# A decoder layer on one core: the second expert's loads moved behind the attention, and the first batch's gate projection moved behind softplus

## The reference

```
xc, res = split(x @ W_in.T + b_in)                  # 512 channels each
u   = silu(conv3(xc) + conv_b)                      # depthwise, causal, 3 taps
dlt, Bm, Cm = split(u @ W_x.T, [64, 80])            # rank 64, 16 states
delta = softplus(dlt @ W_dt.T + b_dt)
h_t = exp(delta * A) * h_(t-1) + delta * u * Bm     # restarts every 64 tokens
x = layernorm(x + ((h . Cm) * silu(res)) @ W_out.T + b_out)
x = layernorm(x + attention(x, ctx, 16 heads of 16))
x = layernorm(x + experts(x))                       # 8 experts: token t of all
                                                    # sequences goes to expert t // 32
experts: (silu(x @ w1) * (x @ w3)) @ w2             # 704 hidden channels
```

## Time and profile before

| | |
|---|---|
| three runs | 2793.26, 2795.64 (median), 2803.66 us |
| profiled execution | 2792.28 us, its span 2790.5 us |
| busy | PE 2424.6, DVE 2140.0, POOL 2074.5, ACT 1802.9 us |
| mean granted TensorE clock | 0.955 |

### The profile page before, as it was taken

The page is one execution under the profiler, slowest core; times in us unless marked ns, Lnnn a source line. Parts: engine busy times, 40 slices in busy tenths (PEclk is TensorE's granted clock), DMA queues, the critical chain, the costliest instruction groups (busy, mean ns, idle before and its releaser), DMA issues. The chain is left out here.

```text
span 2790.5 us, 49779 instructions
## 1 busy us (share of the span) xinstructions
PE 2424.6 (87%) x14816; PEld 1660.6 (60%) x14816; DVE 2140.0 (77%) x3586; ACT 1802.9 (65%) x3972; POOL 2074.5 (74%) x968
## 2 busy tenths in 40 slices
PE   3578888888889898889889888898888879999998
PEld 2345666666666666666666666666665545555554
DVE  1778999999999999999999999999999832322332
ACT  1666777877888888777877787878777541211111
POOL 2999999999999999999999999999999500000000
PEclk8788999999999999999999999999998879999999
DMA  3456566666666666666666666666666360343221
GB/s 118 128 133 149 150 165 168 165 158 157 157 169 166 160 158 165 165 162 168 166 169 164 162 164 166 165 173 163 166 172 158 86 180 12 91 126 96 78 79 31
DMA packets 319323, 399.65 MB, mean 143 GB/s; under 512 B 115697, under 2 KB 256241, under 8 KB 314962
## 3 DMA queue, kind: packets, MB, share of 16 engines
q1 hardware_dynamic: 303698, 384.91, 53.5%
q10 hardware_dynamic: 15360, 11.55, 1.5%
HBM read 300.86 MB, written 94.37 MB: 142 GB/s over the span
## 5 line engine op out<-in xcount | busy, mean ns | idle before, releaser
L506 POOL TENSOR_TENSOR arena<-arena 128x1024 f32<-128x1024 f32 x512 | 1208.2, 2363 | 66.6 <-DMA arena<-w_dram 42.3
L582 ACT ACTIVATE dA_ps<-arena,a_neg 128x252 f32<-128x252 f32 x2048 | 868.7, 461 | 330.4 <-DVE dA_ps L787 172.0
L764 DVE TENSOR_TENSOR_SCAN arena<-dA_ps,arena 128x512 f32<-128x512 f32 x672 | 803.6, 1208 | 112.5 <-ACT dA_ps L582 88.0
L516 POOL TENSOR_TENSOR arena<-arena 128x1024 f32<-128x1024 f32 (+1 forms) x416 | 808.1, 1943 | 17.8 <-DVE arena L764 17.2
L764 DVE TENSOR_TENSOR_SCAN dA_ps<-dA_ps,arena 128x512 f32<-128x512 f32 x352 | 416.2, 1205 | 3.9 <-POOL arena L506 3.7
L887 PE MATMUL a_ps<-xT,w_conv 128*128 128x256 f32 x1536 | 369.8, 391 | 0.0
L829 DVE TENSOR_REDUCE mx<-s_ps 128x2 f32<-128x512 f32 x497 | 334.0, 672 | 23.2 <-PE s_ps L887 23.2
L887 PEld LDWEIGHTS a_ps<-xT,w_conv 128*128 128x128 f32 x1536 | 288.4, 194 | 54.1 <-issue 16.5
L887 PE MATMUL y_ps<-arena,sel 128*32 128x256 f32 x4096 | 257.5, 393 | 55.5 <-DVE m_rows L835 27.8
L640 ACT ACTIVATE probs<-st_ps 128x512 f32<-128x512 f32 x493 | 285.3, 579 | 29.7 <-PE st_ps L887 25.5
L887 PE MATMUL s_ps<-k_st,q_st 96*128 96x256 f32 x994 | 260.6, 344 | 43.7 <-DVE mx L829 28.0
(11 more groups left out here) (111 smaller groups left out, 3272.9 us busy)
## 6 DMA issues: line engine op xcount, KB each, us to landing
arena<-delta_dram SPq DMA_DIRECT2D x512, 128.0 KB, 2.8
arena<-w_dram SPq DMA_DIRECT2D x512, 128.0 KB, 3.2
arena<-bc_dram SPq DMA_DIRECT2D x128, 256.0 KB, 4.5
q_st<-q_parts_dram SPq DMA_DIRECT2D x512, 64.0 KB
k_st<-k_parts_dram SPq DMA_DIRECT2D x512, 64.0 KB
w_dram<-u SPq DMA_DIRECT2D x32, 512.0 KB, 2.8
delta_dram<-delta SPq DMA_DIRECT2D x32, 512.0 KB, 3.8
k_parts_dram<-parts SPq DMA_DIRECT2D x32, 512.0 KB, 4.0
```

What stands on the lines that cost most here:

```text
L506: pool.tensor_tensor(dBu[:, n % NB], w_r[:, n // RP % 2, t % RP].unsqueeze(1).to_broadcast([P, QS, L]), bc_r[:, b.par, 0], ALU.mult).then_ ...
L516: pool.tensor_tensor(h[:, n % NH, states], h[:, n % NH, states], bc_r[:, b.par, 1, states], ALU.mult).then_inc(s_hC, 1)
L582: last = nc.scalar.activation(dA[n % NDA][:, q, :, 1:], delta_r[:, n // (2 * RP) % 2, t % RP].rearrange("p (c t) -> p c t", t=CH)[:, :, 1: ...
L764: nc.vector.tensor_tensor_scan(dst, decays, dBu[:, n % NB, 2 * half:2 * half + 2].rearrange("p q t -> p (q t)"), 0.0, ALU.mult, ALU.add).t ...
```

## The change

Four edits.

1. Start: SP issues the four bias parts ahead of `w_xc` and `conv_rows`. DVE makes `rows * row_scales` first, and the float32r copy is made by ScalarE.
2. Start: `w_x`, `w_dt` and `w_gate` get a semaphore of their own, `s_front`, and are issued ahead of SP's wait. The first `x_proj` waits for them. The wait for the other seven stands ahead of the first `state_sum`.
3. The first batch's `gate_proj` is issued behind its `dt_proj` on TensorE, and its `gate_evac` and Silu behind its `softplus` on ScalarE, with a load of the Exp and Ln table behind it. The other batches are as before.
4. The mixers load expert 0 alone. Expert 1's `w13`, columns, `w2` and rows are issued at the start of the `experts` block, when all stores have landed; its last columns come from DRAM too, and ScalarE copies them for expert 0 only.

```diff
@@ weights and set-up counts
+        front_weights = [(w_x[:], "w_x"), (w_dt[:], "w_dt"), (w_gate[:], "w_gate")]
         weights = [
-            (w_gate[:], "w_gate"), (w_x[:], "w_x"), (w_dt[:], "w_dt"), (sel[:], "sel"), (w_out[:], "w_out"),
+            (sel[:], "sel"), (w_out[:], "w_out"),
...
-        N_CONV = 6 + NDA + TAPS * KD
+        N_ROWS = 3 + NDA
+        N_CONV = 5 + NDA + TAPS * KD
@@ SP
+            for tile, name in bias_parts:
+                sp.dma_start(tile, io[name]).then_inc(s_bias_ld, 16)
             sp.dma_start(w_xc.rearrange("p q t -> p (q t)"), io["w_xc"]).then_inc(s_conv_ld, 16)
             sp.dma_start(conv_rows, io["conv_rows"].partition_broadcast(P)).then_inc(s_conv_ld, 16)
-            for tile, name in bias_parts:
-                sp.dma_start(tile, io[name]).then_inc(s_bias_ld, 16)
 
             def load_weights():
+                for tile, name in front_weights:
+                    sp.dma_start(tile, io[name]).then_inc(s_front, 16)
+                sp.wait_ge(s_const_v, N_SET)
                 for tile, name in weights:
                     sp.dma_start(tile, io[name]).then_inc(s_const, 16)
-                    sp.wait_ge(s_const_v, N_SET)
                 sp.wait_ge(s_const_p, 4)
...
-                    for e in range(2):
-                        shared.load_columns(sp, e, 0, ET - P)
-                        shared.load_rows(sp, e, 0, EJ - 1)
+                    shared.load_columns(sp, 0, 0, ET - P)
+                    shared.load_rows(sp, 0, 0, EJ - 1)
...
-                *[(O_LD + 11 + 6 * e, load_expert(e, shared.load_w13)) for e in range(2)],
-                *[(O_LD + 14 + 6 * e, load_expert(e, shared.load_w2)) for e in range(2)],
+                (O_LD + 11, load_expert(shared.load_w13)),
+                (O_LD + 14, load_expert(shared.load_w2)),
                 (O_LD + 23, load_tokens),
@@ ScalarE
+            act.wait_ge(s_const_v, N_ROWS)
+            nc.scalar.activation(bias[:], rows, ACT.Copy).then_inc(s_const_a, 1)
             nc.scalar.activation(a_neg[:], a_neg[:], ACT.Exp).then_inc(s_const_a, 1)
...
             def silu(b):
                 act.wait_ge(s_conv, b.value(2, 2))
                 nc.scalar.activation(u[:], u[:], ACT.Silu).then_inc(s_u, 1)
-                act.wait_ge(s_gate, b.value(2, 2))
-                nc.scalar.activation(gate[:, b.par], gate[:, b.par], ACT.Silu).then_inc(s_gsilu, 1)
+                if b.back(1):
+                    silu_gate(b)
                 nc.scalar.preload_act_table_set(EXP_LN)
+
+            def first_gate(b):
+                if not b.back(1):
+                    for half in range(2):
+                        gate_evac(half)(b)
+                    silu_gate(b)
+                    nc.scalar.preload_act_table_set(EXP_LN)
...
-                *[(O_GATE + 4 * half + 2, gate_evac(half)) for half in range(2)],
+                *[(O_GATE + 4 * half + 2, later_gate_evac(half)) for half in range(2)],
+                (O_SP + 2, first_gate),
@@ DVE
+            dve.wait_ge(s_bias_ld, 16 * len(bias_parts))
+            nc.vector.tensor_tensor(rows, rows, row_scales, ALU.mult).then_inc(s_const_v, 1)
             dve.wait_ge(s_conv_ld, 32)
...
-            dve.wait_ge(s_const_v, N_CONV - 3)
-            nc.vector.tensor_copy(bias[:], rows).then_inc(s_const_v, 1)
-            dve.wait_ge(s_const_v, N_CONV - 2)
+            dve.wait_ge(s_const_a, 1)
@@ TensorE
-                    if m == 0 and not b.back(1):
-                        pe.wait_ge(s_const, 16 * N_WEIGHTS)
-                        pe.wait_ge(s_const_v, N_SET)
-                        pe.wait_ge(s_const_p, 4)
...
+            def first_gate(b):
+                if not b.back(1):
+                    for m in range(ND):
+                        gate_proj(m)(b)
...
             def x_proj(b):
+                if not b.back(1):
+                    pe.wait_ge(s_front, 16 * len(front_weights))
+                    pe.wait_ge(s_const_v, N_SET)
...
-                *[(O_GATE + 4 * (m // 2), gate_proj(m)) for m in range(ND)],
+                *[(O_GATE + 4 * (m // 2), later_gate(m)) for m in range(ND)],
+                (O_SP + 1, first_gate),
@@ experts, SP
-            for e in range(2):
-                shared.load_rows(sp, e, EJ - 1, EJ)
+            shared.load_rows(sp, 0, EJ - 1, EJ)
             sp.wait_ge(shared.x2T_st, 16 * B)
+            shared.load_w13(sp, 1)
+            for first in range(0, ET, ET // 2):
+                shared.load_columns(sp, 1, first, first + ET // 2)
+            shared.load_w2(sp, 1)
+            for first, last in ((0, EJ - 1), (EJ - 1, EJ)):
+                shared.load_rows(sp, 1, first, last)
```

More of the change, by code:

```diff
@@ L279, in mixers @@
         s_const = sem("weights_loaded")
+        s_front = sem("front_weights_loaded")
         s_const_p = sem("const_set_pool")
@@ L423, in load_stack, with load_expert @@
                 return piece
-            def load_expert(e, load):
+            def load_expert(load):
                 def piece(b):
@@ L429, in piece @@
                         sp.wait_ge(s_sum, ND * B)
-                        load(sp, e)
+                        load(sp, 0)
                 return piece
@@ L446, in load_columns @@
                     sp.wait_ge(s_x2T_st, 16 * (B - 1))
-                    for e in range(2):
-                        shared.load_columns(sp, e, ET - P, ET - EC)
+                    shared.load_columns(sp, 0, ET - P, ET - EC)
             def store_x2T(b):
@@ L547, in gate_evac, with silu_gate @@
                 return piece
+            def silu_gate(b):
+                act.wait_ge(s_gate, b.value(2, 2))
+                nc.scalar.activation(gate[:, b.par], gate[:, b.par], ACT.Silu).then_inc(s_gsilu, 1)
             def silu(b):
@@ L551, in silu, with later_gate_evac, piece @@
                 nc.scalar.activation(u[:], u[:], ACT.Silu).then_inc(s_u, 1)
-                act.wait_ge(s_gate, b.value(2, 2))
-                nc.scalar.activation(gate[:, b.par], gate[:, b.par], ACT.Silu).then_inc(s_gsilu, 1)
+                if b.back(1):
+                    silu_gate(b)
                 nc.scalar.preload_act_table_set(EXP_LN)
+            def first_gate(b):
[4 more added lines that the diff above has]
+                    nc.scalar.preload_act_table_set(EXP_LN)
+            def later_gate_evac(half):
+                def piece(b):
+                    if b.back(1):
+                        gate_evac(half)(b)
+                return piece
             def xp_evac(b):
@@ L663, in x2T_evac @@
                 if b.c == B - 1:
-                    for e in range(2):
-                        nc.scalar.activation(shared.x2T[:, e, :, ET - EC:], a_ps[:, :, EC * e:EC * (e + 1)],
-                                             ACT.Copy).then_inc(shared.last, 1)
+                    nc.scalar.activation(shared.x2T[:, 0, :, ET - EC:], a_ps[:, :, 0:EC],
+                                         ACT.Copy).then_inc(shared.last, 1)
                 nc.scalar.activation(x2T[:], a_ps[:], ACT.Copy).then_inc(s_x2T, 1)
@@ L918, in gate_proj, with later_gate, piece @@
                 return piece
+            def first_gate(b):
+                if not b.back(1):
+                    for m in range(ND):
+                        gate_proj(m)(b)
+            def later_gate(m):
+                def piece(b):
+                    if b.back(1):
+                        gate_proj(m)(b)
+                return piece
             def x_proj(b):
+                if not b.back(1):
+                    pe.wait_ge(s_front, 16 * len(front_weights))
+                    pe.wait_ge(s_const_v, N_SET)
                 pe.wait_ge(s_u, b.value(1, 1))
@@ L940, in piece @@
                     n = b.value(NU, 4 * m)
+                    if m == 0 and not b.back(1):
+                        pe.wait_ge(s_const, 16 * N_WEIGHTS)
+                        pe.wait_ge(s_const_p, 4)
                     pe.wait_ge(s_hC, b.value(len(HC_POOL), sum(t < 4 * m + 4 for t in HC_POOL)))
@@ L1293, in gate_up @@
                 pe.wait_ge(f_xT[b.par], b.same_parity(32))
-                if not b.back(2):
-                    pe.wait_ge(shared.last, b.c + 1)
+                if not b.back(1):
+                    pe.wait_ge(shared.last, 1)
                 pe.wait_ge(f_w13[b.par], b.same_parity(64))
```

4 lines of the change are left out of this document (1 added, 3 removed).

## The result

| | before | after |
|---|---|---|
| six runs each, median | 2794.62 us | 2770.02 us (2767.04 to 2783.80) |
| ratio | | 0.9914, 95% interval 0.9890 to 0.9938 |
| profiled execution, its span | 2792.28, 2790.5 us | 2769.40, 2767.6 us |

The kernel is faster by 24.6 us in the medians and by 22.9 us in the two profiles. The forecast for the median was 2774 with 2765 to 2785, from a gain of 20.

A forecast was written before the change was run, and what follows sets the result against it. GpSimd was taken to pace the batch loop, so only start and drain gain: 16.35 + 3.6 = 19.95 us off 2792.28 gives 2772.3. The median was put 1.7 above the sum, 2774, range 2765 to 2785.

The forecast's parts named there:

- (a): Start, order of the first six loads: later conv_rows takes back the saved cast; 0 us, bounds 3.35 sooner, 0.7 later.
- (b): Start, first batch's gate_proj leaves the chain before x_proj: idle 9.71 and gate halves 4.19 and 2.25 go, 16.15 us.
- (c): Start, ScalarE: the table load follows the u Silu directly, so xp is evacuated sooner; 0.2 us gained.
- (d): Start, moved gate work ends at T + 9.5, hidden before the first decay at T + 14.4; 9.5 us without cover.
- T: Start, the end of softplus, from which the moved gate work is counted; 56.24 us in the kernel before.
- (e): Drain, without expert 1's loads the last row load reaches its matmul in 1.9 us instead of 5.25; 3.35 us gained.
- (f): Drain, one evacuation less ahead of the last x2T copy; 0.23 us gained.
- rival that the row load gets no faster: Drain: the last row load stays slow, taking off the 3.35; 2775.6 us, median 2777; chance 0.13.
- (g): Experts, second expert's loads behind the barrier take 24 us, covered by expert 0's 59 us of matmuls; cost 0.
- the slower rival: Expert 1's first gate_up waits if its loads take over 59 us; at 85 us, 2798 us; chance 0.02.
- Given back in the loop: GpSimd's loop ends less than 16 us earlier; half given back median 2782, all 2790; chance 0.07.

The follow-up runs named there:

- after_rows: Changed kernel with all of expert 0's early loads issued behind the last load of the row maxima; 2766.66 us, ratio 0.9914.
- gate_in_place: Changed kernel, but the first batch's gate work stays between the conv blocks, waiting for the three front weights alone; 2778.46 us.
- drain_only: Kernel before with only the drain's edit, expert 1's loads moved out of the drain; 2789.38 us, ratio 0.9983.
- gate_x3: Changed kernel with 22 more 128x256 products ahead of the first batch's gate work; 2769.42 us.
- after_again: The changed kernel once more, unedited; 2774.10 us, ratio 0.9927.
- old_order: Changed kernel with the first six loads in the old order and DVE's w_conv products ahead of rows * row_scales, cast still on ScalarE; 2765.70 us.
- warm: Changed kernel with seven unread 128x256 products in TensorE's gap between conv(3) and the first x_proj; 2768.44 us.
- start_only: Kernel before with only the start's edits, the drain's loads unchanged; 2781.04 us, ratio 0.9958.
- wdt_split: Kernel before with one edit: w_dt, 97 partitions, loaded as 96 and 1; 2789.84 us, ratio 0.9996.

## Why the prediction was right, step by step

The mechanisms of both parts held, and the measured medians, 2770.0 and again 2774.1, lie around the forecast. Some of the closeness is luck: misses of opposite sign cancelled in part in the start and almost wholly in the drain, as told below, and the first comparison had 3.9 us from the loop besides.

**(a) Order of the first loads: 0 expected.** TensorE started at 15.54 instead of 15.02. `conv_rows` landed at 10.6, 0.6 later than taken, and the rest went as worked out (3.70 + 1.26). The mechanism was right, the size was off by 0.5. The bound of 0.7 later held in this profile and not in others: in `after_rows` TensorE started at 16.25, 1.2 later than in the kernel before.

**(b) The gate off the chain: 16.15.** `gate_in_place` bears out both parts: 9.8 for the wait, 5.3 for the work at the first decay, where 9.71 and 6.44 had been summed. The sizes differ by the clock: a gate half cost 2.25 there at the high level, not 4.19. `x_proj` began at 32.95, forecast 33.75, even though TensorE started 0.5 late, because the clock rose inside the first conv spell (24 matmuls in 6.81 us, where 5.49 + 2.7 had been assumed). What the prediction did not ask is why the ten weights were so late. It was one transfer, and splitting that alone ended 6.6 of the 9.7 us without moving anything. For the same reason the front weights were not "there near 13": in the kernel after one stream of 25 to 27 GB/s still runs from 13 to 17 us. It cost nothing, as `x_proj` came at 32.95.

**(c) 0.2 at `xp`.** Held: `xp`'s copy starts at 36.48, with the last matmul.

**The term that was missing.** The conv spell is followed by 3.3 us in which ScalarE alone works. The prediction carried the old `x_proj` over at 1.97 us. It takes 3.50 with the clock that falls in the gap, and 1.94 with the gap filled. So the start adds up: 16.35, plus 0.8 for the earlier `x_proj` (the clock's 1.3 in the conv spell less the 0.5 of (a)), less 1.5 at `x_proj`, less 0.5 between softplus and the first decay (14.37 before, 14.89 after; the replicated loads were issued 0.4 later behind their stores), is 15.1. The slow `x_proj` is no effect of the change as such. A gap of 3.1 us is in the kernel before too, whose `x_proj` took 1.97 us in one profile and 3.73 in `drain_only`, with the same code. Of the twelve profiles with an unfilled gap, that of the kernel before is the only one below 2.9 us: the forecast had started from the exception.

**(d) The cover.** T + 9.5 forecast, T + 10.0 measured; first decay at T + 14.9 for T + 14.4. The 4.9 us of cover are what `gate_x3` used up. A table load takes 1.28 us in the profile after as well, and the Silu behind it starts 0.02 later (30.34, 31.64). By the 2.66 us that the Trainium skill has for a switch ("ScalarE: Activation LUTs", What ACT_TABLE_LOAD costs) the end would have been an estimated T + 12.3; the trace disagrees with it.

**(e) The row load: 3.35, and (f) 0.23.** The load took 3.73 us less in the profiles (5.25 to 1.52), and (f) gave 0.1 (the `x2T` copy starts 0.12 us behind the start of the one copy left, and started 0.23 behind that of two). The 3.72 for the whole drain also hold two terms that the sum did not have: the load was issued 1.0 us earlier, counted from GpSimd's last product (71.52 to 70.51), and from its matmul to the last copy it took 1.0 longer (21.66 to 22.68), mostly at eight transposes that ran at the low clock there and at the high one before (1.11 and 1.09 us for 0.66 and 0.63; granted 0.50 from 2269, against 1.00 up to 2294). Over the table, without a second expert's data in the drain and with all else as in the change (seven profiles: after, after_again, drain_only, old_order, gate_in_place, warm, gate_x3), the drain is 95.8 us in the mean; with both experts' (before, start_only, wdt_split) 99.4. That is 3.6, the forecast for (e) and (f) together. The rival that the row load gets no faster is out: 4.6 to 5.7 us with the backlog in four profiles, 1.5 to 1.8 without in ten. The margin was thin, though. Expert 0's tokens were to have landed 3 us ahead of the load; in the profile after 96 GB/s still flow from 2258.5 to 2259.0, and the load was issued at 2258.87.

Slow beside a backlog does not mean last in it. In the kernel before SP issued its last large load at 2277.28, ahead of the row load. The matmul that waits for the row load started at 2284.12, and these are the windows of the kernel before from there on (columns as in the earlier trace rows):

```profile
2284.00:2286.00 2.00, 1.88 (x14) 1.10 (x18) 0.00 (x0) 0.60 (x1) 0.00 (x0) 0.50 1.03 399
2286.00:2288.00 2.00, 2.00 (x14) 1.21 (x6) 0.00 (x0) 0.83 (x2) 0.00 (x0) 0.55 1.07 388
```

From 2284 to 2290 1.69 MB move on SP's queue, which got nothing new in that time. So the small load did overtake large loads issued before it, and still took 5.25 us. What exactly it waits for, one packet in each of many rounds or its descriptors, no run tells.

**(g) The second expert.** Its loads were issued from 2287 to 2296, 3 us after the barrier; the forecast allowed 24 us for the whole. They have all landed by 2302, 43 us before expert 1 begins. The 9.5 us read as the pace of a full queue were not that alone: SP also stood in them ahead of an `x2T` store (no issue from 2267.3 to 2269.4), and part of `w2` was issued behind them. The cover was wide enough for either reading, and the slower rival had no ground.

**Given back in the loop.** This rival had the right place and no fixed sign. The loop's instructions are the same in all fourteen kernels, and its length lies between 2124.5 and 2140.5 us. The changed kernel had 2132.86 in one profile and 2136.81 in the other; before had 2136.74. So the 3.9 us of the first comparison, which make its 24.6 us larger than the sum of 20, are best read as chance. The second comparison has 20.4 in the medians. `gate_x3` has the shortest loop with the latest start relative to its loads. GpSimd's first `dBu` products ran ahead of ScalarE there, while xT of batch 1 was issued 3.6 us later (56.36 for 52.79). So part of such a delay may be made up; with one profile that is a guess.

## What to carry to other kernels

A wait for "all weights" should be opened before anything is moved: ask which transfer is last, and by what rate. Here one of ten moved at 26 GB/s for its whole length because of its 97 partitions.

When bulk loads are put into a stretch that seems to have idle DMA engines, look for the smallest transfer on the critical chain there. 8 KB took 1.5 us alone and 4.6 to 5.8 beside a backlog, and the bulk had 43 us to spare one stage later.

A kernel of 2.8 ms that is measured to 0.3% hides edits of 2 to 4 us. Landmarks in the profiles separated them, after the chance of the long loop (4 us between the two profiles of the same changed kernel) was taken out.

## What was unexpected of the hardware

- A transfer of 97 partitions ran as one stream of 26 GB/s; as 96 + 1 it went with the others, at up to 377 GB/s.
- The granted clock in the first conv spell stands as 1.00 in the profile (15 to 21 us, before), while its twelve matmuls took 5.49 us, twice the 2.76 of the same twelve at 35.12, where it is 1.00 too: the pace of the lower level, 1.2 GHz. The column is no evidence there; the durations are.
- TensorE's clock decides some 2.5 us in this start alone: `x_proj` and `dt_proj` together took about 4 us in one execution of the same instructions and about 8 in another (`drain_only`), and softplus ended 3.0 us later there, 0.5 of it from a later `x_proj`.
- An 8 KB load on ScalarE's queue took 5.25 us beside SP's large loads and yet overtook 1.7 MB of them; without them it took 1.5 to 1.8.
